# Attention B's division moved from token rows to feature rows, with DMA copies in place of transpositions

## The reference

```python
x = x + attn_a(layernorm(x))   # linear attention, 16 heads of 64
x = x + ffn(layernorm(x))      # r * (relu(k)^2 @ W_v), token shift
x = x + attn_b(layernorm(x))
x = x + ffn(layernorm(x))

def attn_b(x):                 # 16 heads of 8, rotary positions
    q, k, v = proj(W_Q), proj(W_K), proj(W_V)
    q, k = rope(q), rope(k)
    attn = softmax(einsum('bhqd,bhkd->bhqk', q, k) / sqrt(8))
    return einsum('bhqk,bhkd->bhqd', attn, v) @ W_O.T
```

## Time and profile before

| | |
|---|---|
| median of 3 runs | 1062.75 us (1061.67 to 1063.92) |
| the profiled execution | 1061.35 us, span 1059.6 us |
| TensorE busy | 970.6 us (92%) |
| ScalarE, VectorE, GpSimd busy | 773.4 us (73%), 630.9 us (60%), 422.1 us (40%) |
| granted TensorE clock, mean | 0.977 of full speed |
| chain that ended last, TensorE's share | 67% |

### The profile page before, as it was taken

One profiled execution on the slowest core, in us unless ns is written; L12 is line 12 of the kernel. 1 busy time (PEld: TensorE's weight loads), 2 busy tenths in 40 slices (PEclk: granted clock), 3 DMA queues, 4 the chain that ended last, 5 costly groups with the idle time before them and its releaser, 6 DMA issues.

```text
span 1059.6 us, 21453 instructions
## 1 busy us (share of the span) xinstructions
PE 970.6 (92%) x8311; PEld 534.4 (50%) x8311; DVE 630.9 (60%) x1520; ACT 773.4 (73%) x895; POOL 422.1 (40%) x306
## 2 busy tenths in 40 slices
PE   5987989999999999999999999999999999898983
PEld 3775435455554545545454554545454554443332
DVE  5666536575565657565564756656465755675332
ACT  4655776878788787868778787877878787676870
POOL 4757252624434362534335262542526234223000
PEclk9998999999999999999999999999999999998995
DMA  5002212223131222323122222312222231322210
GB/s 171 26 13 92 59 60 66 75 61 100 50 97 44 72 64 63 96 56 96 40 71 71 66 85 60 101 31 81 66 66 70 61 91 44 97 57 84 70 41 15
DMA packets 61938, 72.25 MB, mean 68 GB/s; under 512 B 12289, under 2 KB 38786, under 8 KB 61826
## 3 DMA queue, kind: packets, MB, share of 16 engines
q1 hardware_dynamic: 61826, 70.75, 23.3%
HBM read 16.19 MB, written 20.97 MB: 35 GB/s over the span
## 4 chain that ended last, share of the span: by engine, by line
PE 67%; DVE 12%; ACT 12%; issue 5%; POOL 2%; SPq 1%; DMA 1%; ACTq 0%; DVEq 0%; POOLq 0%
PE PS L1437 17%; PE PS L1254 8%; PE PS L1393 7%; PE PS L1256 5%; PE PS L1255 5%; PE PS L1249 5%; PE PS L1310 4%; ACT work L585 4%; PE PS L1354 3%; PE PS L1361 3%; PE PS L1331 3%; PE PS L1348 2%; ACT hn L612 2%; ACT k_relu L621 1%; ACT gate L626 1%
## 5 line engine op out<-in xcount | busy, mean ns | idle before, releaser
L585 ACT ACTIVATE work<-PS 128x2048 f32<-128x2048 f32 x208 | 390.6, 1878 | 0.8 <-PE PS L1393 0.4
L1437 PE MATMUL PS<-work,v 128*32 128x512 f32 x2048 | 275.9, 611 | 6.4 <-DVE U L959 5.9
L579 ACT ACTIVATE work<-PS 128x512 f32<-128x512 f32 x256 | 152.0, 597 | 176.9 <-PE PS L1256 174.7
L384 POOL TENSOR_TENSOR rs<-ve,half_neg 128x4 f32<-128x4 f32 x64 | 65.3, 1020 | 367.8 <-DVE ve L806 367.8
L397 POOL TENSOR_TENSOR work<-work,q_rcp 128x1024 f32<-128x1024 f32 x64 | 121.9, 1904 | 146.7 <-DVE q_rcp L858 146.7
L1254 PE MATMUL PS<-wqk,h1h 128*128 128x512 f32 x256 | 121.8, 476 | 25.5 <-ACT gate L626 13.4
L1393 PE MATMUL PS<-q_st,k_st 32*128 32x512 f32 x832 | 106.1, 499 | 0.1
L1256 PE MATMUL PS<-wqk,h1l 128*128 128x512 f32 x256 | 102.3, 400 | 0.0
L1255 PE MATMUL PS<-wqk,h1h 128*128 128x512 f32 x256 | 101.8, 397 | 0.0
L1310 PEld LDWEIGHTS PS<-work 128*64 128x64 f32 x2048 | 65.4, 138 | 42.5 <-ACT work L579 33.9
L855 DVE TENSOR_REDUCE q_sum<-work 128x16 f32<-128x1024 f32 x64 | 77.7, 1213 | 12.4 <-ACT work L579 11.9
(11 more groups left out here) (149 smaller groups left out, 1645.3 us busy)
## 6 DMA issues: line engine op xcount, KB each, us to landing
qkv_scratch<-qkv_sb SPq DMA_DIRECT2D x16, 768.0 KB, 3.6
k_st<-k_hi SPq DMA_DIRECT2D x128, 64.0 KB, 2.1
k_st<-k_lo SPq DMA_DIRECT2D x128, 64.0 KB, 2.1
q_st<-q_hi SPq DMA_DIRECT2D x128, 64.0 KB, 2.1
q_st<-q_lo SPq DMA_DIRECT2D x128, 64.0 KB, 2.1
xa<-in_attn_a_x SPq DMA_DIRECT2D x16, 256.0 KB, 3.0
xr<-in_attn_a_x SPq DMA_DIRECT2D x16, 256.0 KB, 2.9
x_scratch<-x SPq DMA_DIRECT2D x16, 256.0 KB, 2.0
```

The costliest lines, as they stand in the source:

```text
L384: pool.tensor_tensor(rs[:, :], ve[:, :], half_neg[:, :], ALU.pow).then_inc(rstd[n].sem, 1)
L579: act.activation((EQ, EK)[r // 2][c % 2][:, (r % 2) * 512:(r % 2) * 512 + 512], PS[:, bank, :], ACT.Exp)\
L585: act.activation(probs[n % 2], PS[:, 0:4, :], ACT.Exp).then_inc(z["s_exp"].sem, 1)
L1437: mm = pe.matmul(PS[32 * h:32 * h + 32, 6, :], v_flat[p][:, kc, at:at + 32], probs[n % 2][:, h, :], start=(n % 8 == 0), stop=(n % 8 == 7), ...
```

## The change

In `v32` a one now stands beside every value column: values in the even columns, ones in the odd ones, of the 16 used. So `weigh_values`, whose instructions stay the same in number and size, leaves value rows on the even partitions and, below each, a row with the sum. Four DMA transfers a batch (`part_values`, 64 rows of 2 KB each, 128 KB) bring the value rows of both halves to `parted[:, 0, :]` and the sums to `parted[:, 1, :]`, on the same 128 partitions. `divide` (DVE) then takes the reciprocal of 128x512 sums and multiplies, straight into `cT`. Gone are both `u_transposes`, `c_transposes`, both `normalise` and `cT_copy` (the functions stay for the second path, which this input does not take). `ctx_wout` in slot 2 now waits for `split_h3`, and some other waits on `u_norm` and `ct_sb` are replaced by others.

```diff
+        parted = sb("parted", [P, 2, N])
...
+            def part_values(z, j, u):
+
+                if u == 0:
+                    hold(sp, z["ct_sb"], j - 1)
+                hold(sp, z["pv_sb"], j, u + 1)
+                for t in range(2):
+                    sp.dma_start(parted[64 * u:64 * u + 64, t, :], U[u][t:P:2, :]).then_inc(z["c_in"].sem, 16)
...
                     stack_k(z, b, 1)
                     stack_q(z, b, 1)
+                if there(e):
+                    part_values(z, e, 1)
+                if there(b):
                     stack_k(z, b, 2)
                     stack_q(z, b, 2)
...
                     stack_k(z, b, 3)
                     stack_q(z, b, 3)
+                    part_values(z, b, 0)
...
-                pool.tensor_tensor(v32[p][:, :, :, 0:DB], qkv_sb[:, :, 2 * D:W3].rearrange("p c (h d) -> p c h d", h=HB),
+                pool.tensor_tensor(v32[p][:, :, :, 0:2 * DB:2], qkv_sb[:, :, 2 * D:W3].rearrange("p c (h d) -> p c h d", h=HB),
...
-                    pool.memset(v32[t][:, :, :, DB:DB + 1], 1.0).then_inc(v0_ok.sem, 1)
+                    pool.memset(v32[t][:, :, :, 1:2 * DB:2], 1.0).then_inc(v0_ok.sem, 1)
...
-                    if n == 2 and E:
-                        cT_copy(z, e)
...
+            def divide(z, j):
+                hold(dve, z["c_in"], j)
+                dve.reciprocal(parted[:, 1, :], parted[:, 1, :]).then_inc(z["c_rcp"].sem, 1)
+                hold(dve, z["c_rcp"], j)
+                hold(dve, z["o_mm"], j - 1)
+                dve.tensor_tensor(cT[:, :], parted[:, 0, :], parted[:, 1, :], ALU.mult).then_inc(z["ct_sb"].sem, 1)
...
-                if E:
-                    normalise(z, e, 1)
...
+                if E:
+                    divide(z, e)
                 if there(a + 1):
                     ln1_stats(a + 1)
...
-                if B:
-                    normalise(z, b, 0)
...
-                        if E and n == 3:
-                            hold(pe, z["ct_sb"], e)
...
                     if n == 0 and L and at.h3T == 0:
-                        hold(pe, z["u_norm"], e, 2)
+                        hold(pe, f1["x"], s - 1, 1)
+                        hold(pe, f2["x"], e - 1, 1)
                         h3_transposes(l)
-                    if n == 1 and E:
...
-                        u_transposes(z, e, 1)
-                    if n == 2 and E:
...
-                        c_transposes(z, e)
                     if n == 2 and S:
                         if E:
-                            hold(pe, z["u_norm"], e)
+                            hold(pe, h3_sp, l)
...
-                        u_transposes(z, b, 0)
```

More of the change, by code:

```diff
@@ L210, in hybrid_block @@
                 ("k_in0", 128), ("k_in1", 128), ("q_in0", 128), ("q_in1", 128),
-                ("s_mm", 16), ("s_exp", 16), ("pv", 16), ("pv_sb", 2), ("u_T", 2), ("u_norm", 4),
+                ("s_mm", 16), ("s_exp", 16), ("pv", 16), ("pv_sb", 2), ("c_in", 64), ("c_rcp", 1), ("u_T", 2), ("u_norm", 4),
                 ("ct_ps", 1), ("ct_sb", 1), ("o_mm", 1), ("x2_in", 16), ("x3_ok", 1), ("out_st", 16))})
@@ L957, in pv_copy @@
                 hold(dve, z["pv"], b, 8 * u + 8)
-                hold(dve, z["u_T"], b, u - 1)
+                if z is att[0]:
+                    hold(dve, z["c_in"], b - 1)
+                else:
+                    hold(dve, z["u_T"], b, u - 1)
                 dve.tensor_copy(U[u][:, :], PS[:, 6, :]).then_inc(z["pv_sb"].sem, 1)
@@ L964, in normalise @@
                 hold(dve, z["u_T"], b, u + 1)
-                dve.reciprocal(den_rcp[:, :, :], src[:, :, :, DB]).then_inc(z["u_norm"].sem, 1)
+                dve.reciprocal(den_rcp[:, :, :], src[:, :, :, 1]).then_inc(z["u_norm"].sem, 1)
                 hold(dve, z["u_norm"], b, 2 * u + 1)
                 dve.tensor_tensor(c_tok[:, :, 64 * u:64 * u + 64].rearrange("p c (h d) -> p c h d", h=8),
-                                  src[:, :, :, 0:DB], den_rcp[:, :, :].unsqueeze(3).to_broadcast([P, NC, 8, DB]),
+                                  src[:, :, :, 0:2 * DB:2], den_rcp[:, :, :].unsqueeze(3).to_broadcast([P, NC, 8, DB]),
                                   ALU.mult).then_inc(z["u_norm"].sem, 1)
+            def divide(z, j):
[4 more added lines that the diff above has]
+                dve.tensor_tensor(cT[:, :], parted[:, 0, :], parted[:, 1, :], ALU.mult).then_inc(z["ct_sb"].sem, 1)
             def add_x3(z, n, j):
@@ L1605, in fused @@
                             hold(pe, t_ev, s)
-                        elif n == at.pb:
-                            hold(pe, z["u_norm"], e)
                         proj_b(l, n - at.pb)
@@ L1617, in fused @@
                     if n == 6 and at_batch(i, NB + 2):
-                        hold(pe, z["ct_sb"], e)
+                        hold(pe, f2["gate"], e - 1)
                         norm_transposes()
@@ L1641, in fused @@
                         else:
-                            hold(pe, z["ct_sb"], e)
+                            hold(pe, ph_exp, NB - 1)
+                            hold(pe, f2["gate"], e - 1)
                         ffn_k(f1, s)
```

9 lines of the change are left out of this document (removed).

## The result

The changed kernel takes 1057.37 us (median of 4 runs, 1056.37 to 1057.45) against 1063.14 us before (4 runs, 1061.67 to 1063.92): a ratio of 0.9945, 95% interval 0.9928 to 0.9962. It is faster by 5.8 us. Forecast were 11.2 us; the time lies inside the range of 1044 to 1061, but 1.4 us outside the forecast's own of 1047 to 1056. The sign was right, and so was the mechanism of the full steps; the draining steps lost nearly twice what was forecast, in part by a mechanism that the prediction did not have.

The account below looks back on a forecast made before the run. TensorE was taken to bound the full steps, with VectorE on the path in the draining steps. -18.0 + 6.8 = -11.2 us gave a forecast of 1051.5 us (own range 1047 to 1056), overall range 1044 to 1061.

Parts of the forecast that it names:

- Full steps: TensorE without its transposition groups gains 0.61 + 0.41 + 0.49 = 1.5 us a step, 18.0 us over 12 steps.
- Rivals 2 and 3: Full steps: gain partly hidden, 1056 to 1060.6 us, chance 0.14; or transpositions were covered, no gain, 1064.6 us, chance 0.06.
- rival 2: Full steps: ScalarE's exponentials or a late VectorE take half the gain, 1056 to 1060.6 us; chance 0.14.
- VectorE at zero in the full steps: The added division fits into VectorE's idle time in the full steps and costs them nothing.
- slack of 1.7 us: VectorE can be 1.7 us later than computed before a full step gets longer.
- Reciprocal: VectorE's reciprocal of 128x512 takes 3353 ns, from the slope of two small ones; upper end 4.5 us.
- Landing: The new 128 KB transfers land 2.4 us after issue, between 2.1 for 64 KB and 3.6 for 768 KB.
- Draining steps: Steps 16 to 19, with VectorE on the path, lose 6.8 us together; bounds +1.3 to some +13.
- step 16: Division between second p_copy and add_x1 costs 3.65 us, TensorE comes 1.9 us earlier: net +1.8 us.
- step 17: Division delays heads_out and add_x3 by 2.6 us, transpositions give about 1.0 us: net +1.6 us.
- step 18: Transpositions give about 1.1 us, a late cT takes back 0.5: -0.6 us.
- step 19: Program's end, nothing beside it: pv_copy to heads_out takes 7.15 us in place of 3.17, +4.0 us.

Follow-up runs that it names:

- no_divide: Changed kernel without the DMA transfers and the reciprocal, the output operand being the product of the two copied halves: 1042.31 us, ratio 0.9793.
- no_recip: Changed kernel with the transfers and the product but without the reciprocal: 1045.41 us, ratio 0.9822.
- before_plus_divide: Kernel before, transpositions kept and used, with the new value layout, transfers, reciprocal and product added, their result unused: 1072.12 us, ratio 1.008.
- two_recips: Changed kernel with a second, unused reciprocal of 128x512 in each of the twelve full steps: 1077.04 us, ratio 1.0142.
- rope_held: Changed kernel with GpSimd's rotary products in the draining steps held until VectorE's norms are done: 1049.04 us, ratio 0.9869.
- before_rope_held: Kernel before with GpSimd's rotary products in the draining steps held until VectorE's norms are done: 1057.48 us, ratio 0.9949.

## Why the prediction was right, and where it was not

- **Full steps, forecast -18.0, measured -16.3** (12 x 1.36; 16.56 by the two `ctx_hd`). Slot 1 gave the 0.61 us worked out, and ScalarE limited it as said. The other two slots gave 0.40 and 0.38 in place of 0.49 and 0.41: slot 2's scores are now 413.80 - 410.13 = 3.67 us from slot 3's, and were 4.07. I had counted a group from start to start, but part of that time was the next group's: `ctx_wout`'s first part now takes 0.32 us to its next start, not 418.97 - 418.76 = 0.21. Rivals 2 and 3 fall with the step of 59.63 us: 16.3 of 18.0 us were kept. The time itself, 1057.4, lies in the band that I had given to rival 2 (1056 to 1060.6), whose mechanism did not occur.
- **VectorE at zero in the full steps: right.** no_divide, no_recip and before_plus_divide leave their steps' lengths as they were. My slack of 1.7 us was too generous: two_recips shows 1.1.
- **Reciprocal: right.** 3353 ns from the slope of two small ones, 3348 measured. The Trainium skill's repeat count of 8 ("VectorE: DVE Perf Modes", "First, the fixed hardware budget"), which by my estimate made 4.3 us, is not what an element costs here; the measurement decides.
- **Landing: 2.8 us, taken as 2.4,** inside its bounds; at the program's end it is most of what step 19 cost beyond the forecast.
- **Draining steps, forecast +6.8, measured +12.0: the step that failed.** By term: step 16 +1.8, measured +4.96; step 17 +1.6, measured 2.3; step 18 -0.6, measured +0.2; step 19 +4.0, measured 4.6. The division cost 3.5 us in step 16, near the 3.65 worked out, but the gain set against it was 1.2 us, not 1.9, and 2.5 us (5.77 - 3.28) came from the collision of the norms with GpSimd's rotary products, for which the sum had no term. I had looked for such a collision at `divide`'s own product, where none occurred, and not at the instructions that `divide` pushes back. rope_held and before_rope_held show it: with the products held in both kernels, the draining loss is 6.7 us in the traces, 7.9 by the medians. That 6.7 is so near the forecast of 6.8 is luck: by step it is +2.4, +2.7, -2.9 and +4.4, where +1.8, +1.6, -0.6 and +4.0 stood. The granted clock, 0.88 and 0.89 where it was 0.92 and 0.93, is in all these numbers; no run separates it.
- On that collision the Trainium skill speaks more fully in "SBUF — State Buffer", "Who interferes with whom": there a VectorE copy or `tensor_scalar` can enter a mode that needs the port pair it shares with GpSimd, and whichever begins first keeps it for its whole instruction. I had drawn on the rule for two SBUF inputs alone. The norms are of the `TENSOR_SCALAR` form, with one tensor input, and they do stall, so the trace agrees.
- **Step 17** lost 3.2 us between the second `p_copy` and `add_x3` (forecast 2.6); the 0.6 us beyond came because `heads_out` ran 1.64 us in place of 1.05 after a wait of 2.18 us, at a granted clock of 0.89 between 928 and 974 us.
- **The range held, but not for its reasons.** It reached up to 1061 for the rivals' sake, not for a loss of 12 us in the draining steps, and the medians lie 1.7 us further apart than the traces explain (5.8 and 4.1), which brought the time nearer to the forecast. The errors of the two terms, +1.7 and +5.2, both went the same way.

Of the signs that I had named, the missing groups, the step, the reciprocal, VectorE's two waits and the 7 us at the end came as said. The landing lay 0.1 us above its range, and the draining steps lost 12.0 us, past the 10 that I had set as a mark of being wrong.

## What to carry to other kernels

Price a stage by what ends its waits there: a reciprocal of 3.35 us that is free in twelve steady steps cost 3 us a time, on average, in the four last ones, nearly its full length. And what is removed from one engine must be set against both. When an instruction is put in ahead of others, walk the instructions behind it to their new places in time and see what they meet there on the neighbouring engine, and, when it is moved forward, look at what it waits for and what is queued behind that. An end without anything beside it can keep the old, shorter chain.

## What the hardware showed

- `TENSOR_SCALAR` norms of 128x128 that take 0.34 us alone are held by consecutive GpSimd products, one norm by each: eight in 6.66 us beside three products of 5.3 us in all, 2.13 us when these start behind them; in step 17 four norms beside four products took 6.44 us. Two waits added on GpSimd were worth 5.2 us on the kernel before and 8.3 on the changed one.
- A reciprocal of f32 costs 6.25 ns for each further element of a partition, from 8 to 16 (203 to 253 ns) and on to 512 (3353 ns, the median of 16).
- A transfer of 64 rows of 2 KB from SBUF to SBUF lands 2.8 us after its issue (64 transfers), those of 64 KB after 2.1.
